# Three-layer compressed interaction network on one core: the field products in four strips of 32 rows instead of two halves of 64, two of them in banks of y

## The chip, the cores and the metric

The kernel runs on one core of a Trainium2 chip. The metric is the device time of one execution in microseconds; before the change its median over three runs is 1070.07 us (1069.95 to 1070.9). The core has five engines that run their own queues and wait for each other by semaphores: TensorE (matmuls, PE in the profile, its weight loads PEld), VectorE (DVE), ScalarE (ACT), GpSimd (POOL) and SyncE (SP, which issues most DMAs). Matmuls write to PSUM, which has eight banks of 512 f32 values a partition; VectorE and ScalarE read and write it.

## The reference

```python
# r_input: (512, 64, 16) = batch, fields, embedding; W0: (128, 64*64); W1, W2: (128, 128*64)
x_vec = input
outs = []
for W, b in [(W0, b0), (W1, b1), (W2, b2)]:
    z = einsum('bhd,bfd->bhfd', x_vec, input)      # every row of x_vec times every field
    z = z.reshape(B, h * f, d)
    x_vec = einsum('oc,bcd->bod', W, z) + b[None, :, None]
    outs.append(x_vec.sum(axis=2))                 # sum over the embedding
return concatenate(outs, axis=1)                   # (512, 384)
```

All values are float32.

## The kernel before

**Tiles.** A column is a pair of batch element and embedding place. A tile is 128 columns (TILE_B = 8 batch elements of 16 places), a group is four tiles, and there are 16 groups, so 64 tiles. `body` runs once for the first group, in a sequence for the 14 inner groups, and once for the last.

**Layer 0** (`layer0`) makes l0 = W0 z for a whole group in 17 steps t. z, the products of fields, is made by GpSimd (`product`) from copies that DMAs lay down shifted. Nine of the steps are "in parts" (PARTED): z is split in an upper part (ScalarE, `part_upper`) and a remainder (VectorE, `part_lower`), and three fast matmuls take the place of a two-pass one. The steps of group n+1 are done while group n is in layer 1: AHEAD_AT lists behind which of the group's 64 chunks each stands, PARTED_AT when ScalarE and VectorE split.

**Layer 1** is the bulk. For each tile TensorE makes 16 chunks (`chunk`): chunk c holds the products of the tile's columns with W1 for four fields (CF = 4), 512 values a partition, in three matmuls of 512 columns (`by_parts`). A chunk lands in one of five banks y[0..4], taken in turn: chunk c of a tile waits until chunk c - 5 has been taken out. Taking out means: multiply each field's 128 columns by the field's value of the column and add. There are three ways. A chunk in SUMMED is done by VectorE in four multiply-adds into acc (`add_fields`). A chunk in SCALED is multiplied in place by ScalarE (`scale`, four activations) and added by VectorE in one step. A chunk in HELPED is multiplied by ScalarE into prod (`multiply`) and added up by GpSimd in pacc (`add_products`). HELPED is (1, 4, 6, 8, 12), SCALED (3,), and (3, 9) in the last four tiles. After the tile GpSimd adds acc and pacc to x2 (`combine`), in the last tile VectorE does.

**Field products.** For layer 2 the kernel doesn't form z again. For each tile it makes gram, for every batch element the products of x2's rows with the fields, summed over the embedding. The columns of a batch element must not mix, so `own_rows` lays the fields in bd once per batch element of a half, zero where a column isn't its own: HALF_B = 4 copies of 64 columns by four activations, and 4 columns more for the plain sums. `layer2` is two f32 matmuls, rows 0 to 63 and rows 64 to 127 of the tile, each 260 columns wide, into the two banks l2p[0] and l2p[1]. It is done for tile - 1 behind chunk LAYER2_AT = 13 of a tile. ScalarE copies both banks out with one copy to gram and one to sums1 (`layer2_out`, behind chunk 14's place). Every 16 tiles `quarter` multiplies gram by W2 on TensorE; the last quarter comes at the end of the kernel.

**Order.** Nothing plans: every engine's order is the program's, by the index e = 16 j + c of a chunk in its group. ScalarE also copies W2 in 16 parts (`keep_w2`, at chunk indices 78, 89, ... 243 of the kernel). At the end TensorE keeps busy with 24 transposes, waits for x2 of tile 63, makes its field products and the last quarter.

Of the kernel before, what the change touches and what calls it, by code (L numbers as in the profile page):

```python
# [7 lines left out]
ALU = mybir.AluOpType  # L8
# [5 lines left out]
O = 128  # L14
# [5 lines left out]
HALF = P // 2  # L20
HALF_B = TILE_B // 2
# [44 lines left out]
OWN_AT = 11  # L66
GRAM = HALF_B * F

# [4 lines left out]
LOWER_AT = 3  # L73
# [15 lines left out]
LATER_AT = [3 + t * 11 // ZT for t in range(ZT)]  # L89
# [3 lines left out]
LATER_PRODUCTS = (6, (3, 0, 5, 3, 0))  # L93
AHEAD_AT = [8 + t * 46 // (ZT - 1) for t in range(ZT)]
# [22 lines left out]
def cin_kernel(nc, x, w0, b0, w1, b1, w2, b2, out):  # L117
    with ExitStack() as ctx:
        def sb(name, shape, dt=F32):
            return ctx.enter_context(nc.sbuf_tensor(name, shape, dt))  # L120
# [23 lines left out]
        bd = sb("bd", [P, 2, GRAM + HALF_B])  # L144
# [6 lines left out]
        own_half = sb("own_half", [P, HALF_B])  # L151
# [32 lines left out]
        beside = GRAM + HALF_B  # L184
# [331 lines left out]
        def _(act):  # L516
# [150 lines left out]
            def own_rows(tile, j):  # L667
# [17 lines left out]
            def multiply(tile, j, c):  # L685
# [36 lines left out]
            nc.scalar.copy(gram[:, :, QB - TILE_B:QB - HALF_B], l2p[:, 0, 0:GRAM].rearrange("p (b f) -> p f b", f=F))  # L722
            nc.scalar.copy(sums1[:, B - TILE_B:B - HALF_B], l2p[:, 0, GRAM:GRAM + HALF_B]).then_inc(l2p_used, 1)
# [5 lines left out]
        def _(dve):  # L729
# [37 lines left out]
            def add_fields(tile, j, c):  # L767
# [4 lines left out]
                if c in scaled_in(tile):  # L772
# [3 lines left out]
                    nc.vector.tensor_tensor(to, y[(CHUNKS * tile + c) % YB][:], to, ALU.add).then_inc(acc_step, 1)  # L776
# [141 lines left out]
            for k in range(W1_AHEAD):  # L918
# [14 lines left out]
            nc.vector.tensor_copy(gram[:, :, QB - HALF_B:QB],  # L933
                                  l2p[:, 1, 0:GRAM].rearrange("p (b f) -> p f b", f=F)).then_inc(gram_half_made, 1)
# [251 lines left out]
```

## Time and profile before

| | us |
|---|---|
| median of three runs | 1070.07 |
| lowest, highest | 1069.95, 1070.9 |
| the profiled execution | 1069.11 |
| its span, first to last instruction | 1067.4 |
| TensorE busy | 1049.3 |
| VectorE busy | 916.8 |
| GpSimd busy | 874.4 |
| ScalarE busy | 672.8 |
| granted TensorE clock, mean | 1.000 |

Busy means that at least one instruction of the engine was on its way. The rows stand in a section of their own below. In a row of a timeline come the start in us from the span's start, the duration in us, the engine, the line, the operation, what it writes and reads, and how many records were merged; in brackets the idle time of the engine ahead of it and the engine and line that ended it. The lines that matter: L951 are the three matmuls of a chunk (and of a step in parts), L972 a whole step of layer 0, L1065 the field products, L1147 the transposes that keep TensorE busy, L1158 the last quarter, L1051 the other quarters, L791 VectorE's multiply-add, L776 its one-step sum of a scaled chunk, L814 a bias step on sums0, L693 ScalarE's multiply into prod, L682 its scale in place, L672 the rows of `own_rows`, L581 and L722 its copies to gram, L615 the copy of W2.

### The profile page before, as it was taken

Reading aid. Unit: us, or ns where it says so; the run is one execution under the profiler, and the core shown is the slowest. Engines: PE = TensorE matmul, PEld = TensorE weight load, DVE = VectorE, ACT = ScalarE, POOL = GpSimd, SP = SyncE. Lnnn points to the kernel's source line nnn. Section 1 sums busy time; section 2 is a strip of 40 time slices with the busy share of each in tenths; the row PEclk is TensorE's granted clock in tenths of the full one; section 3 lists DMA queues with packets and bytes.
Section 4 is the critical chain, followed back from the end, with each engine's and each line's share of the span. In section 5 each row is a group of like instructions: output and inputs, shape, how many; then the busy total and the mean of one; then the engine's idle time right before and its main releaser. Section 6 shows DMA issues by size and latency. Waiting matters only on the chain.

```text
span 1067.4 us, 18145 instructions
## 1 busy us (share of the span) xinstructions
PE 1049.3 (98%) x4764; PEld 803.3 (75%) x4764; DVE 916.8 (86%) x2874; ACT 672.8 (63%) x2253; POOL 874.4 (82%) x727
## 2 busy tenths in 40 slices
PE   6999999999999999999999999999999999999998
PEld 6866777777787777777778777777778877777777
DVE  5988989898966999989993898989997599998983
ACT  4756677786744756666563665767565475766771
POOL 2789998989886898989985899898988589898660
PEclk9999999999999999999999999999999999999999
DMA  7443435354321433223141241423332133331000
GB/s 280 102 120 86 112 84 130 87 119 107 80 61 48 85 84 77 80 59 98 50 105 43 40 112 53 97 80 70 100 77 60 47 70 92 75 79 41 1 24 8
DMA packets 124105, 85.96 MB, mean 81 GB/s; under 512 B 87585, under 2 KB 90625, under 8 KB 123873
## 3 DMA queue, kind: packets, MB, share of 16 engines
q1 hardware_dynamic: 105968, 74.04, 28.8%
q10 hardware_dynamic: 18032, 10.75, 3.3%
q8 instruction: 38, 0.62, 0.2%
q14 instruction: 67, 0.54, 0.2%
HBM read 14.81 MB, written 0.79 MB: 15 GB/s over the span
## 4 chain that ended last, share of the span: by engine, by line
PE 89%; DVE 4%; POOL 3%; issue 2%; DMA 1%; ACT 1%; ACTq 0%; DVEq 0%; POOLq 0%
PE y L951 60%; PE l L951 9%; PE l L972 9%; PE l2p L1051 4%; PE l2p L1065 3%; DVE acc L791 3%; PE l2p L1158 1%; DMA gram<-in_L_rec_W_dram 1%; POOL z L465 1%; POOL pacc L475 1%; PE l2p L1006 1%; POOL pacc L473 1%; PE l2p L1029 1%; POOL pacc L481 0%; ACT y L682 0%
## 5 line engine op out<-in xcount | busy, mean ns | idle before, releaser
L791 DVE SCALAR_TENSOR_TENSOR acc<-y,x0t,acc 128x128 f32<-128x128 f32 x2288 | 619.8, 339 | 90.2 <-PE y L951 86.6
L693 ACT ACTIVATE prod<-y,x0t 128x128 f32<-128x128 f32 x1280 | 368.0, 379 | 284.9 <-PE y L951 221.8
L951 PE MATMUL y<-w1h,x1h 128*128 128x512 f32 x1024 | 451.1, 440 | 2.9 <-issue 1.5
L951 PE MATMUL y<-w1h,x1l 128*128 128x512 f32 x1024 | 400.6, 391 | 0.0
L951 PE MATMUL y<-w1l,x1h 128*128 128x512 f32 x1024 | 399.9, 390 | 0.0
L465 POOL TENSOR_TENSOR z<-z,xg 128x512 f32<-128x512 f32 (+2 forms) x272 | 361.5, 1334 | 22.0 <-DMA z<-xg 22.0
L475 POOL TENSOR_TENSOR pacc<-pacc,prod 128x512 f32<-128x512 f32 x192 | 271.0, 1412 | 68.5 <-ACT prod L693 64.4
L951 PEld LDWEIGHTS y<-w1h,x1h 128*128 128x128 f32 x1024 | 192.9, 188 | 77.5 <-DVE acc L791 19.8
L951 PEld LDWEIGHTS y<-w1l,x1h 128*128 128x128 f32 x1024 | 192.6, 188 | 59.2 <-issue 25.2
L951 PEld LDWEIGHTS y<-w1h,x1l 128*128 128x128 f32 x1024 | 192.2, 188 | 42.0
L740 DVE TENSOR_TENSOR zl<-z,zh 128x512 fp32r<-128x512 f32 (+1 forms) x144 | 144.3, 1003 | 5.4 <-ACT zh L542 5.2
L473 POOL TENSOR_TENSOR pacc<-prod 128x512 f32<-128x512 f32 x64 | 85.5, 1336 | 37.8 <-ACT prod L693 37.3
L972 PE MATMUL l<-z,w0t 128*128 128x512 f32 (+1 forms) x224 | 114.4, 592 | 0.0
L481 POOL TENSOR_TENSOR pacc<-pacc,acc 128x512 f32<-128x512 f32 x63 | 86.8, 1378 | 31.1 <-DVE acc L791 30.8
L542 ACT CAST zh<-z 128x512 fp32r<-128x512 f32 (+1 forms) x144 | 90.7, 630 | 13.3 <-POOL z L465 12.7
L682 ACT ACTIVATE y<-y,x0t 128x128 f32<-128x128 f32 x272 | 76.4, 351 | 14.7 <-PE y L951 14.7
L672 ACT ACTIVATE bd<-x0t,own_half 128x64 f32<-128x64 f32 x256 | 69.7, 373 | 1.0 <-ACT w2t L615 1.0
L776 DVE TENSOR_TENSOR acc<-y,acc 128x512 f32<-128x512 f32 x68 | 46.8, 688 | 24.3 <-ACT y L682 23.4
L951 PE MATMUL l<-zh,w0h 128*128 128x512 f32 (+1 forms) x144 | 58.8, 408 | 1.3 <-DVE zl L740 1.3
L483 POOL TENSOR_TENSOR pacc<-pacc 128x256 f32<-128x256 f32 x63 | 55.4, 880 | 4.9
L951 PE MATMUL l<-zl,w0h 128*128 128x512 f32 (+1 forms) x144 | 55.8, 388 | 0.0
L951 PE MATMUL l<-zh,w0l 128*128 128x512 f32 (+1 forms) x144 | 55.8, 387 | 0.0
(102 smaller groups left out, 698.5 us busy)
## 6 DMA issues: line engine op xcount, KB each, us to landing
z<-xg SPq DMA_DIRECT2D x480, 128.0 KB, 2.4
w2t<-in_L_rec_W_dram ACTq DMA_DIRECT2D x8, 512.0 KB, 10.3
sums<-in_L_rec_W_dram ACTq DMA_DIRECT2D x16, 256.0 KB, 4.0
xg<-in_r_input_dram SPq DMA_DIRECT2D x30, 128.0 KB, 3.9
z<-xg SPq DMA_DIRECT2D x32, 96.0 KB, 2.2
z<-xg SPq DMA_DIRECT2D x15, 192.0 KB
gram<-in_L_rec_W_dram ACTq DMA_DIRECT2D x1, 2048.0 KB, 10.4
out_dram<-z SPq DMA_DIRECT2D x3, 192.0 KB, 1.9
```

The costliest lines, as they stand in the source:

```text
L465: nc.gpsimd.tensor_tensor(to[0:rows, :], to[0:rows, :], xg[0:rows, cols], ALU.mult).then_inc(z_made, 1)
L473: nc.gpsimd.tensor_tensor(pacc[:], prod[:, 0], prod[:, 1], ALU.add).then_inc(pool_step, 1)
L475: nc.gpsimd.tensor_tensor(pacc[:], pacc[:], prod[:, h % HSLOTS], ALU.add).then_inc(pool_step, 1)
L481: nc.gpsimd.tensor_tensor(pacc[:], pacc[:], acc[:, slot], ALU.add).then_inc(pool_step, 1)
L542: nc.scalar.copy(zh[:, slot, cols], zin(n, t)).then_inc(zh_made, 1)
L672: last = nc.scalar.activation(bd[:, j % 2, b * F:(b + 1) * F], x0t[:, j, :], ACT.Copy, scale=own_half[:, b:b + 1])
L682: last = nc.scalar.activation(of, of, ACT.Copy, scale=x0t[:, j, f:f + 1])
L693: last = nc.scalar.activation(prod[:, h % HSLOTS, k, :], y[(CHUNKS * tile + c) % YB][:, k * O:(k + 1) * O], ACT.Copy, scale=x0t[:, j, f:f ...
L740: nc.vector.tensor_tensor(zl[:, i % ZLSLOTS, cols], zin(n, t), zh[:, zhslot(n, t), cols].bitcast(F32), ALU.subtract).then_inc(zl_made, 1)
L791: ins = nc.vector.scalar_tensor_tensor(out=to, in0=of, scalar=x0t[:, j, f:f + 1], in1=b1r[:] if m == 0 else to, op0=ALU.mult, op1=ALU.add)
L951: ins = nc.tensor.matmul(to, stationary, moving, start=(first and k == 0), stop=(last and k == 2))
L972: nc.tensor.matmul(l0[:, cols], w0t[:, WHOLE.index(t), :], zin(n, t), start=(t == 0), stop=False).then_inc(z_used, 1)
```

## The change

The tile is cut in four strips of 32 rows (STRIPS, STRIP, STRIP_B = 2) where it was cut in two halves. bd is 2 x 64 + 2 = 130 columns wide and `own_rows` makes two copies in place of four, now at chunk 4 (OWN_AT) in place of 11. `layer2` issues four matmuls of 32 rows and 130 columns: the first two into l2p[0] and l2p[1], the others into two banks of y. These two count as turns in y's rotation, so a tile has 18 turns: 14 chunks, two strips, two chunks. `ybank`, `turn_of`, `strip_turns` and `user_ahead` work out whose turn a bank had before, and `turn_free` is the wait for it. `layer2_out` copies the strips out in three pairs of copies in place of one. In the last tile ScalarE copies two strips and VectorE two.

The rest is a new deal: HELPED becomes (0, 4, 6, 9, 12), SCALED (3, 11) and (3,) in the last group. Lists of places follow (AHEAD_AT, AHEAD_FIRST_AT, LATER_AT, PARTED_FIRST_AT, PRODUCTS_AT, LOWER_AT), with nine steps in parts as before. AHEAD_AT was 8, 10, 13, 16, 19, 22, 25, 28, 31, 33, 36, 39, 42, 45, 48, 51, 54 and becomes 10, 12, 15, 18, 21, 24, 26, 29, 32, 35, 38, 40, 43, 46, 49, 52, 55; the last of LATER_AT goes from 13 to 14.

```diff
-HALF = P // 2
-HALF_B = TILE_B // 2
+STRIPS = 4
+STRIP = P // STRIPS
+STRIP_B = TILE_B // STRIPS
-HELPED = (1, 4, 6, 8, 12)
+HELPED = (0, 4, 6, 9, 12)
-SCALED = (3,)
-SCALED_LAST = (3, 9)
+SCALED = (3, 11)
+SCALED_LAST = (3,)
-OWN_AT = 11
-GRAM = HALF_B * F
+OWN_AT = 4
+GRAM = STRIP_B * F
-LOWER_AT = 3
+LOWER_AT = 2
-LATER_AT = [3 + t * 11 // ZT for t in range(ZT)]
+LATER_AT = [3 + t * 12 // ZT for t in range(ZT)]
-LATER_PRODUCTS = (6, (3, 0, 5, 3, 0))
-AHEAD_AT = [8 + t * 46 // (ZT - 1) for t in range(ZT)]
+LATER_PRODUCTS = (5, (3, 0, 5, 4, 0))
+AHEAD_AT = [10 + t * 45 // (ZT - 1) for t in range(ZT)]
-AHEAD_FIRST_AT = [26 + t * 29 // (ZT - 1) for t in range(ZT)]
+AHEAD_FIRST_AT = [27 + t * 28 // (ZT - 1) for t in range(ZT)]
-PARTED_FIRST_AT = [{AHEAD_FIRST_AT[t] - k: t for t in PARTED} for k in (5, 3)]
+PARTED_FIRST_AT = [{AHEAD_FIRST_AT[t] - k: t for t in PARTED} for k in (5, 4)]
-PRODUCTS_FIRST_AT = ((0, 0, 0, 0, 0), (0, 3, 1, 0, 1), (3, 3, 1, 1, 4), (0, 0, 0, 0, 0))
-PRODUCTS_AT = ((2, 1, 1, 1, 1), (1, 1, 1, 1, 1), (1, 1, 1, 1, 1), (1, 0, 0, 0, 0))
+PRODUCTS_FIRST_AT = ((0, 0, 0, 0, 0), (0, 4, 1, 1, 1), (3, 2, 1, 1, 3), (0, 0, 0, 0, 0))
+PRODUCTS_AT = ((2, 1, 1, 1, 1), (2, 1, 1, 1, 1), (1, 1, 1, 1, 1), (0, 0, 0, 0, 0))
...
+        Y_STRIPS = STRIPS - 2
+        TURNS = CHUNKS + Y_STRIPS
+        def turn_of(tile, c):
+            return TURNS * tile + c + (Y_STRIPS if c > LAYER2_AT else 0)
+        def ybank(tile, c):
+            return turn_of(tile, c) % YB
+        def strip_turns(tile):
+            first = TURNS * tile + (LAYER2_AT + 1 if tile < GROUPS * TILES else 0)
+            return range(first, first + Y_STRIPS)
+        def user_ahead(turn):
+            tile, at = divmod(turn - YB, TURNS)
+            if LAYER2_AT < at <= LAYER2_AT + Y_STRIPS:
+                return (tile, None) if tile > 0 else user_ahead(turn - YB)
+            return tile, at - (Y_STRIPS if at > LAYER2_AT else 0)
...
             def layer2_out(tile, to):
-                nc.scalar.copy(gram[:, :, bass.ds(to, TILE_B)].rearrange("p f (k b) -> p f k b", k=2),
-                               l2p[:, :, 0:GRAM].rearrange("p k (b f) -> p f k b", f=F))
-                nc.scalar.copy(sums1[:, bass.ds(tile * TILE_B, TILE_B)].rearrange("p (k b) -> p k b", k=2),
-                               l2p[:, :, GRAM:GRAM + HALF_B]).then_inc(l2p_used, 1)
+                parts = [(0, l2p[:], 2)]
+                parts += [(2 + i, y[turn % YB][:].unsqueeze(1), 1) for i, turn in enumerate(strip_turns(tile + 1))]
+                for at, of, k in parts:
+                    b = at * STRIP_B
+                    nc.scalar.copy(gram[:, :, bass.ds(to + b, k * STRIP_B)].rearrange("p f (k b) -> p f k b", k=k),
+                                   of[:, :, 0:GRAM].rearrange("p k (b f) -> p f k b", f=F))
+                    last = nc.scalar.copy(
+                        sums1[:, bass.ds(tile * TILE_B + b, k * STRIP_B)].rearrange("p (k b) -> p k b", k=k),
+                        of[:, :, GRAM:GRAM + STRIP_B])
+                last.then_inc(l2p_used, 1)
...
             def own_rows(tile, j):
-                for b in range(HALF_B):
+                for b in range(STRIP_B):
...
+            def turn_free(turn):
+                user, c = user_ahead(turn)
+                if c is None:
+                    pe.wait_ge(l2p_used, user + 1)
+                elif user < 0:
+                    return
+                elif c in HELPED:
+                    pe.wait_ge(prod_made, HN * user + HN + HELPED.index(c) + 1)
+                else:
+                    pe.wait_ge(acc_step, added(user, c))
...
             def layer2(tile, slot, fields_kept, quarters_out):
-                for k in range(2):
-                    half = slice(k * HALF, (k + 1) * HALF)
-                    last = nc.tensor.matmul(l2p[:, k, 0:GRAM + HALF_B], x2[half, slot], bd[half, slot, :],
+                turns = strip_turns(tile + 1)
+                for turn in turns:
+                    turn_free(turn)
+                for k, to in enumerate([l2p[:, 0], l2p[:, 1]] + [y[turn % YB][:] for turn in turns]):
+                    rows = slice(k * STRIP, (k + 1) * STRIP)
+                    last = nc.tensor.matmul(to[:, 0:GRAM + STRIP_B], x2[rows, slot], bd[rows, slot, :],
                                             start=True, stop=True)
                 last.then_inc(l2p_made, 1)
             def chunk(tile, j, c):
-                before, late = (c - YB) % CHUNKS, c < YB
-                if before in HELPED:
-                    value = HN * tile + (HN + HELPED.index(before) + 1) - (HN if late else 0)
-                    pe.wait_ge(prod_made, value)
-                else:
-                    pe.wait_ge(acc_step, added(tile - 1 if late else tile, before))
+                turn_free(turn_of(tile, c))
```

## Rows read from the trace of the kernel before

**Rows 1.** The page, busy time, share of the span and instructions of each engine

```profile
PE 1049.3 (98%) x4764; PEld 803.3 (75%) x4764; DVE 916.8 (86%) x2874; ACT 672.8 (63%) x2253; POOL 874.4 (82%) x727
```

**Rows 2.** The page, the chain that ended last, by engine and by line

```profile
PE 89%; DVE 4%; POOL 3%; issue 2%; DMA 1%; ACT 1%; ACTq 0%; DVEq 0%; POOLq 0%
PE y L951 60%; PE l L951 9%; PE l L972 9%; PE l2p L1051 4%; PE l2p L1065 3%; DVE acc L791 3%; PE l2p L1158 1%; DMA gram<-in_L_rec_W_dram 1%; POOL z L465 1%; POOL pacc L475 1%; PE l2p L1006 1%; POOL pacc L473 1%; PE l2p L1029 1%; POOL pacc L481 0%; ACT y L682 0%
```

**Rows 3.** Groups by line and form: busy us, mean ns, then idle before

```profile
L791 DVE SCALAR_TENSOR_TENSOR acc<-y,x0t,acc 128x128 f32<-128x128 f32 x2288 | 619.8, 339 | 90.2 <-PE y L951 86.6
L951 PE MATMUL y<-w1h,x1h 128*128 128x512 f32 x1024 | 451.1, 440 | 2.9 <-issue 1.5 <-DVE acc L791 0.9 <-ACT prod L693 0.3
...
L672 ACT ACTIVATE bd<-x0t,own_half 128x64 f32<-128x64 f32 x256 | 69.7, 373 | 1.0 <-ACT w2t L615 1.0
...
L1051 PE MATMUL l2p<-gram,w2t 128*128 128x128 f32 x384 | 46.7, 275 | 0.0
...
L581 ACT COPY gram<-l2p 128x512 f32<-128x512 f32 x63 | 37.4, 594 | 12.1 <-PE l2p L1065 11.5 <-ACT w2t L615 0.4
...
L615 ACT COPY w2t<-sums 128x512 f32<-128x512 f32 x16 | 18.6, 1164 | 0.0
```

**Rows 4.** Timeline, TensorE and ScalarE around one tile's field products, in narrow windows

```profile
511.09 0.39 PE L951 MATMUL y<-w1h,x1l 128*128 128x512 f32 x1
511.40 0.49 PE L1065 MATMUL l2p<-bd,x 64*128 64x260 f32 x2
511.73 0.39 PE L1065 MATMUL l2p<-bd,x 64*128 64x260 f32 x2
...
512.16 0.59 ACT L581 COPY gram<-l2p 128x512 f32<-128x512 f32 x1 [0.35 <-PE l2p L1065]
512.38 0.39 PE L951 MATMUL y<-w1l,x1h 128*128 128x512 f32 x1
```

**Rows 5.** Timeline, last thirds of two chunks and the multiply one releases

```profile
540.82 0.39 PE L951 MATMUL y<-w1h,x1l 128*128 128x512 f32 x1
...
541.25 1.15 ACT L693 ACTIVATE prod<-y,x0t 128x128 f32<-128x128 f32 x4 [0.40 <-PE y L951]
...
541.50 0.39 PE L951 MATMUL y<-w1h,x1l 128*128 128x512 f32 x1
```

**Rows 6.** Timeline, a scaled chunk of the last tile, all three engines

```profile
1039.85 0.39 PE L951 MATMUL y<-w1h,x1l 128*128 128x512 f32 x1
...
1040.09 1.14 ACT L682 ACTIVATE y<-y,x0t 128x128 f32<-128x128 f32 x4
...
1041.25 0.69 DVE L776 TENSOR_TENSOR acc<-y,acc 128x512 f32<-128x512 f32 x1 [1.35 <-ACT y L682]
```

**Rows 7.** Timeline, TensorE waiting for a bank early in the last group

```profile
999.75 1.14 DVE L814 TENSOR_SCALAR sums<-sums,b0d 128x512 f32<-128x512 f32 x1
1000.81 1.11 DVE L791 SCALAR_TENSOR_TENSOR acc<-y,x0t,acc 128x128 f32<-128x128 f32 x4
...
1001.98 0.50 PE L951 MATMUL y<-w1h,x1h 128*128 128x512 f32 x1 [0.88 <-DVE acc L791]
...
1002.31 0.39 PE L951 MATMUL y<-w1l,x1h 128*128 128x512 f32 x1
```

**Rows 8.** Busy time of each engine (records) in group 14 and last group

```profile
933.90:994.10 60.20, 60.20 (x255) 45.09 (x254) 55.93 (x179) 39.62 (x136) 54.79 (x45) 1.00 0.20 54
994.10:1044.30 50.20, 49.17 (x218) 37.26 (x217) 44.37 (x153) 38.38 (x141) 30.33 (x28) 1.00 0.04 13
```

**Rows 9.** Timeline, the end of the last tile

```profile
1042.05 5.26 DVE L791 SCALAR_TENSOR_TENSOR acc<-y,x0t,acc 128x128 f32<-128x128 f32 x20
...
1044.10 0.40 PE L951 MATMUL y<-w1h,x1l 128*128 128x512 f32 x1
...
1048.94 0.71 PE L1065 MATMUL l2p<-bd,x 64*128 64x260 f32 x4 [1.83 <-DVE x L929]
1049.70 0.37 ACT L722 COPY gram<-l2p 128x256 f32<-128x256 f32 x1 [5.93 <-PE l2p L1065]
```

More of the change, by code:

```diff
@@ L183, in cin_kernel @@
         l2p = ps("l2p", [P, 2, CHUNK])
-        beside = GRAM + HALF_B
+        beside = GRAM + STRIP_B
         l2 = l2p[:, 0, beside:beside + QB]
@@ L680, in scale @@
                     f = CF * c + k
-                    of = y[(CHUNKS * tile + c) % YB][:, k * O:(k + 1) * O]
+                    of = y[ybank(tile, c)][:, k * O:(k + 1) * O]
                     last = nc.scalar.activation(of, of, ACT.Copy, scale=x0t[:, j, f:f + 1])
@@ L692, in multiply @@
                     f = CF * c + k
-                    last = nc.scalar.activation(prod[:, h % HSLOTS, k, :], y[(CHUNKS * tile + c) % YB][:, k * O:(k + 1) * O],
+                    last = nc.scalar.activation(prod[:, h % HSLOTS, k, :], y[ybank(tile, c)][:, k * O:(k + 1) * O],
                                                 ACT.Copy, scale=x0t[:, j, f:f + 1])
@@ L721, in _ @@
             act.wait_ge(l2p_made, layer2_ready(GROUPS * TILES - 1))
-            nc.scalar.copy(gram[:, :, QB - TILE_B:QB - HALF_B], l2p[:, 0, 0:GRAM].rearrange("p (b f) -> p f b", f=F))
-            nc.scalar.copy(sums1[:, B - TILE_B:B - HALF_B], l2p[:, 0, GRAM:GRAM + HALF_B]).then_inc(l2p_used, 1)
+            nc.scalar.copy(gram[:, :, QB - TILE_B:QB - 2 * STRIP_B].rearrange("p f (k b) -> p f k b", k=2),
+                           l2p[:, :, 0:GRAM].rearrange("p k (b f) -> p f k b", f=F))
+            nc.scalar.copy(sums1[:, B - TILE_B:B - 2 * STRIP_B].rearrange("p (k b) -> p k b", k=2),
+                           l2p[:, :, GRAM:GRAM + STRIP_B]).then_inc(l2p_used, 1)
             act.wait_ge(turned, B // P)
@@ L775, in add_fields @@
                     to = acc[:, j % 2].rearrange("p k o -> p (k o)")
-                    nc.vector.tensor_tensor(to, y[(CHUNKS * tile + c) % YB][:], to, ALU.add).then_inc(acc_step, 1)
+                    nc.vector.tensor_tensor(to, y[ybank(tile, c)][:], to, ALU.add).then_inc(acc_step, 1)
                     return
@@ L781, in add_fields @@
                     f = CF * c + k
-                    to, of = acc[:, j % 2, k, :], y[(CHUNKS * tile + c) % YB][:, k * O:(k + 1) * O]
+                    to, of = acc[:, j % 2, k, :], y[ybank(tile, c)][:, k * O:(k + 1) * O]
                     if after_scaled and k == 0:
@@ L837, in _ @@
             dve.wait_ge(consts_made, 1)
+            by_strip = own[:].rearrange("p (k b) -> p b k", b=STRIP_B)
             for slot in range(2):
-                nc.vector.tensor_tensor(bd[:, slot, GRAM:GRAM + HALF_B], own[:, 0:HALF_B], own[:, HALF_B:TILE_B], ALU.add)
-            nc.vector.tensor_tensor(own_half[:], own[:, 0:HALF_B], own[:, HALF_B:TILE_B], ALU.add).then_inc(own_made, 1)
+                nc.vector.tensor_reduce(bd[:, slot, GRAM:GRAM + STRIP_B], by_strip, AX.X, ALU.add)
+            nc.vector.tensor_reduce(own_strip[:], by_strip, AX.X, ALU.add).then_inc(own_made, 1)
             dve.wait_ge(x_turned, 1)
@@ L932, in _ @@
             dve.wait_ge(l2p_made, layer2_ready(tile))
-            nc.vector.tensor_copy(gram[:, :, QB - HALF_B:QB],
-                                  l2p[:, 1, 0:GRAM].rearrange("p (b f) -> p f b", f=F)).then_inc(gram_half_made, 1)
-            nc.vector.tensor_copy(sums1[:, B - HALF_B:B], l2p[:, 1, GRAM:GRAM + HALF_B]).then_inc(gram_half_made, 1)
+            strip_banks = [y[turn % YB] for turn in strip_turns(tile + 1)]
+            for i, of in enumerate(strip_banks):
+                at = QB - (Y_STRIPS - i) * STRIP_B
+                last = nc.vector.tensor_copy(gram[:, :, at:at + STRIP_B],
+                                             of[:, 0:GRAM].rearrange("p (b f) -> p f b", f=F))
+            last.then_inc(gram_half_made, 1)
+            for i, of in enumerate(strip_banks):
+                at = B - (Y_STRIPS - i) * STRIP_B
+                last = nc.vector.tensor_copy(sums1[:, at:at + STRIP_B], of[:, GRAM:GRAM + STRIP_B])
+            last.then_inc(gram_half_made, 1)
             dve.wait_ge(b2r_made, 1)
```

8 lines of the change are left out of this document (4 added, 4 removed).

## The prediction

> **What bounds the kernel now.** I read the page's busy shares, then the chain of waits, then the groups by line, then timelines of single tiles. TensorE is busy 98% of the span at a granted clock of 1.00 and carries 89% of the chain; VectorE is at 86% [rows 1, 2]. Busy time alone isn't proof, so look at the idle column: before the 1024 first matmuls of the chunks TensorE idled 2.9 us in all, and the clean groups of sixteen chunks are 60.2 us of 60.2 busy [rows 3, 8]. From tile 4 on, the time is the sum of what TensorE streams. A third of a chunk takes 0.227 us (541.50 less 540.82, over three) [rows 5], a chunk 0.68 us. VectorE fills 55.9 of 60.2 us of such a group and ScalarE 39.6 [rows 8]: neither ends last, but VectorE has only 4.3/4 = 1.1 us of slack a tile. So the change can gain only by shortening the TensorE stream, and it loses wherever TensorE comes to wait.
>
> **Field products (`layer2`), 64 times.** Before, they are two matmuls of 64 rows and 260 columns, four records each time (two passes a matmul). What they cost is read from the starts: the last third of the chunk before starts at 511.09 and would end at 511.32; the second third of the next chunk starts at 512.38 where 511.55 would be its undisturbed start: 0.83 us [rows 4]. Its parts: 0.08 us until the first weights load (511.32 to 511.40), about 0.10 us of load that nothing covers (the first pair reads 0.49 us, the second 0.39) [rows 4], then two pairs of passes, then the same two gaps on the way back. The two halves run side by side: two records start within one printed hundredth at 511.40, two at 511.73 [rows 4], and ScalarE's copy starts at 512.16, 0.43 us behind the second pair's start. From an ordinary third, 540.82, to the multiply that it releases, 541.25, it is 0.43 as well [rows 4, 5], so the second pair streams no longer than an ordinary third and nothing is queued behind it. Two pairs take 0.83 - 4 x 0.10 = 0.43 us, 0.217 each for 260 columns.
>
> After, four matmuls of 32 rows and 130 columns. If all four strips run side by side, there are again two waves, of 130 columns: 0.108 each, 0.22 together; the load for the second wave (0.10) just fits under the first. The gain is 0.21 us a time. Bounds: nothing at all, if only two strips run at once (four waves of 0.108); a loss of 0.50 if the eight passes ran singly, at 46.7/384 = 0.12 us for a pass of 128 columns [rows 3], which the pairs of [rows 4] speak against. Issue isn't the limit as far as a row shows it: the records of a pair start together [rows 4]. I take 0.21, the row nearest in kind: 64 x 0.21 = **-13.4 us**. The Trainium skill (TensorE: Matmul & The Clock Gate, "Measured speedup vs the span model") gives four row strips 3.07 times the speed of one after another, not 4; by that the waves would be 8 x 0.108/3.07 = 0.28 us, an estimate, and the sum 4 us less of a gain. No row here shows four strips, and the sum leaves it out.
>
> **Banks of y.** This is the price. The last two strips take two turns of the five banks between chunks 13 and 14. Chunk 14 then needs chunk 11 out of its bank (before: 9), chunk 15 needs 12, the next tile's chunk 0 needs 13, and the products need 9 and 10. Queued behind such a wait is all of TensorE. From the end of chunk 11's stream to chunk 14's lie two chunks and the products: 0.68 + 0.68 + 0.62 = 1.98 us. Chunk 11 is now scaled in ScalarE and added in one VectorE step. Its consumption is priced from such a chunk of the last tile: third started 1039.85, stream end 1040.08, scale starts at 1040.09 when ScalarE was late, or 0.20 behind the stream's end when it is free (0.43 less 0.23) [rows 5, 6]; from scale start to the end of the sum 1041.94 - 1040.09 = 1.85. So 0.20 + 1.85 = 2.05. The release itself, read at the one stall of the last group: VectorE ends at 1001.92, the next third starts at 1001.98 and its second at 1002.31, so it really streamed from 1002.08: 0.16 [rows 7]. Chunk 14 can stream at 2.21 behind chunk 11 where it could at 1.98: a stall of 0.2 us, unless a step of the first layer lies between. The new list AHEAD_AT puts one behind chunks 12 (tile 0 of a group), 13 (tile 1) and 11 (tile 2), each 0.68 us or more, and none behind chunk 7 of tile 3. So 15 tiles pay: 15 x 0.2 = **+3 us**. The other new limits hold by my working of tile 3: chunk 9 (1.35 behind its end by rows of 1.15 us a multiply plus 0.20), 10 (1.6 behind, by laying VectorE's steps in program order from chunk 13 of tile 2 on; limit 2.0), 13 (limit 1.98 + 0.2) and the strips themselves: ScalarE's six copies, 1.1 us by an estimate from 0.59 for 512 columns and 0.37 for 256 [rows 3, 9], end 2.2 us behind chunk 13's end, against 2.8 for chunk 1 of the next tile.
>
> **ScalarE.** It adds a scaled chunk (1.14 us) [rows 6], saves two of the four rows of `own_rows` (69.7/256 = 0.27 each) and gets 0.35 us more of copies: +0.95 us in a tile of 15, on an engine at 66% [rows 3, 8]: hidden. Not hidden are the sixteen 1.16 us copies of W2 (L615) [rows 3] where one meets a tight chunk without a step behind it. They fall at indices 78, 89, ... 243: index 122 is chunk 10 of a tile 3, ahead of the scaled chunk 11 (1.1 us late), and 188 is chunk 12 of a tile 3 (0.8 us); the other fourteen meet a step of layer 0 or a wait of full depth. **+1.9 us**; 0 to 6 as bounds.
>
> **VectorE and GpSimd.** VectorE saves four steps of 619.8/2288 = 0.27 and adds one of 0.69: -0.4 us a tile [rows 3, 6]. No time by itself; it is why chunk 10 is soon free. GpSimd does the same 17 products and five sums a tile; the sum of the first two still waits for chunk 4, while its slot is now wanted at chunk 9 instead of 8, so that wait shrinks. The extra waits in TensorE's queue (two) are hidden: its sequencer passes them ahead of the stream.
>
> **First and last group.** In tile 0 the last step of layer 0 moves from behind chunk 13 to behind chunk 14, and with it the values that tile 1 starts on; against it, VectorE has 0.4 us less a tile there. I take +0.5, bounds -1.5 and +2.5. The last group has no steps of layer 0: 64 chunks and four products stream 46 us, and VectorE needs 4 x (10 x 1.07 + 0.65) + 2 = 47.4 us. Before, the 50.2 us of [rows 8] less 43.5 and 3.3 left 3.4 us for row turns and stalls, 1.1 of it at chunk 10 of its first tile, behind the bias step of 1.14 us [rows 7]. With a tighter rotation I put 0.5 on top. But VectorE then ends nearer behind the last chunk: chunk 11 can be 1.8 us behind at most (1.98 less the release), and by 1.07 a chunk 15 is then some 1.9 behind. Before, VectorE ended at 1047.31, 3.0 us behind the last chunk's stream (1044.33), and TensorE waited 1.83 us for x2 [rows 9]: -1.1. The second copies of the last two strips cost under 0.1.
>
> **Sum.** -13.4 + 3.0 + 1.9 + 0.5 + 0.5 - 1.1 = -8.6 us. The profiled execution took 1069.11 us (span 1067.4), 0.96 under the median of the runs; from it the sum gives 1060.5, and put on the median 1070.07 - 8.6 = **1061.5 us**.
>
> **Rivals.** (a) Two strips at a time. Two records start at once in this trace, never three [rows 4]. Then the products cost 0.83 as before, the 13.4 is gone and the +4.8 of the rest stays: 1074.9 us, slower. It decides as soon as fewer than some 0.08 us a tile are gained. The Trainium skill (TensorEngine Tiling (Array Packing), "Tiling Modes") lists four tiles of 32 rows by 128 columns as working independently; by that rule this rival falls, and nothing in this trace can show it. (b) Full concurrency, but the short rotation stalls every tile, not the last of each group alone, because VectorE (93% of a group) comes late to chunks 10 and 13 when its steps for layer 0 lie there: 49 more tiles x 0.19 = 9.3, 1070.8 us, no change. For it speaks that VectorE was 3.0 us behind the last chunk [rows 9]; against it that it has 0.4 us less to do and a step of layer 0 stands in each of these places. (c) No stall at all: chunk 11's sum keeps up, 1061.5 - 4.9 - 0.5 = 1056 us.
>
> **Chances.** Forecast 0.56 (1059 to 1066), (c) 0.12, (b) 0.17, (a) 0.15. The likeliest one's time is the prediction. The range reaches from just under (c), 1055.5, to just under (a), 1074.0; it leaves out most of (a), some 0.13, and some 0.04 below. A measurement of this kernel tells 0.2% (2.1 us) from no change. Faster than 1067.9: the forecast, (c) and 0.02 of (b), 0.70. Within: 0.12 of (b). Slower: (a) and 0.03 of (b), 0.18.
>
> **What would show it.** In the changed trace the eight records of a tile's products start in two bunches of four about 0.11 us apart, and next chunk's second third is back 0.21 us sooner, with 0.62 us for the whole. Four bunches of two mean rival (a). Idle time before the first third of chunk 14, in tile 3 of a group alone, of 0.2 us and released by VectorE's one-step sum, shows the bank price; in all tiles, rival (b). A clean group should last 60.2 - 0.84 + 0.2 = 59.6 us. The last products' wait for x2 should fall from 1.8 to about 0.7 us. The prediction is wrong if the strips don't overlap, if strips' copies hold chunk 1, or if the retimed first group loses more than 2.5 us.

## The result and the profile after

The changed kernel takes 1080.42 us (median of four runs, 1079.6 to 1080.92) against 1070.01 us of the kernel before (median of four runs). The ratio is 1.0099, 95% interval 1.0087 to 1.0112: about 1% slower, and outside the range that was given (1055.5 to 1074.0 us). The profiled execution took 1079.6 us.

| | before | after |
|---|---|---|
| span, us | 1067.4 | 1077.8 |
| TensorE busy | 1049.3 | 1042.3 |
| VectorE busy | 916.8 | 923.4 |
| ScalarE busy | 672.8 | 708.2 |
| GpSimd busy | 874.4 | 867.2 |

The page first: busy times and the chain by engine, which answer to [rows 1, 2]. (The shares of the chain add up to 78% here, so they are a rough guide.)

```profile
PE 1042.3 (97%) x5020; PEld 803.1 (75%) x5020; DVE 923.4 (86%) x2708; ACT 708.2 (66%) x2601; POOL 867.2 (80%) x727
...
PE 61%; DVE 13%; issue 4%; ACT 0%; POOL 0%; DVEq 0%; ACTq 0%
```

TensorE has 7 us less to do and carries 61% of the chain where it carried 89%; VectorE went from 4% to 13%. VectorE issues 166 instructions fewer and is busy 7 us longer. The groups by line and form say where (busy us, mean ns):

```profile
L772 DVE TENSOR_TENSOR zl<-z,zh 128x512 fp32r<-128x512 f32 x135 | 157.5, 1167 | 1.7 <-ACT zh L566 1.7
...
L780 DVE TENSOR_TENSOR zh<-z,zh 32x512 fp32r<-32x512 f32 x15 | 20.0, 1334 | 0.5
```

These are `part_lower` and `left_lower`, the same instructions as before, where they took 1012 and 1002 ns:

```profile
L740 DVE TENSOR_TENSOR zl<-z,zh 128x512 fp32r<-128x512 f32 x135 | 136.6, 1012 | 3.8 <-ACT zh L542 3.7
...
L748 DVE TENSOR_TENSOR zh<-z,zh 32x512 fp32r<-32x512 f32 x15 | 15.0, 1002 | 0.5
```

Who held TensorE up (waited for: us in total, times, longest; counted from the modelled end of the matmul before, so a little less than by the starts used below):

```profile
PE l L1000 <- DVE zh L780: 13.3, 10, 1.4
PE y L991 <- DVE acc L808: 4.8, 11, 1.4
```

L1000 is layer 0's last step, L808 VectorE's one-step sum of a scaled chunk. A clean group and the last one, as in [rows 8]:

```profile
946.00:1007.50 61.50, 59.90 (x271) 45.04 (x270) 56.21 (x166) 42.26 (x160) 54.69 (x45) 1.00 0.18 48
1007.50:1056.20 48.70, 47.86 (x235) 37.68 (x235) 46.53 (x168) 33.82 (x133) 30.82 (x29) 1.00 0.04 13
```

The group lasts 61.5 us, TensorE has 59.9 us of work in it. The last group is 1.5 us shorter than before.

**What went as forecast.** The field products, which answer to [rows 4], with the thirds of chunks around them:

```profile
500.77 0.39 PE L991 MATMUL y<-w1h,x1l 128*128 128x512 f32 x1
501.09 0.38 PE L1120 MATMUL l2p<-bd,x 32*128 32x130 f32 x2
501.11 0.38 PE L1120 MATMUL y<-bd,x 32*128 32x130 f32 x2
501.31 0.28 PE L1120 MATMUL l2p<-bd,x 32*128 32x130 f32 x2
501.32 0.28 PE L1120 MATMUL y<-bd,x 32*128 32x130 f32 x2
501.53 0.50 PE L991 MATMUL y<-w1h,x1h 128*128 128x512 f32 x1
501.86 0.39 PE L991 MATMUL y<-w1l,x1h 128*128 128x512 f32 x1
```

The eight records come in two bunches of four, all four strips at once. The bunches start 0.22 us apart and not 0.11 as the prediction's sign had it: that figure left out the 0.10 us of weight load that its own sum counts. The next chunk's second third starts at 501.86 where 501.23 would be undisturbed (500.77 plus two thirds of 0.227): 0.63 us, 0.20 less than 0.83. (In the clean groups the products cost 0.84 us before and 0.63 to 0.65 us now, in whichever tile they stand.)

**What did not.** In tile 3 of a group TensorE stands still for 1.56 us: a third starts at 419.71 and is streamed by 419.94, and the step behind it starts at 421.50. VectorE, GpSimd and TensorE in one stretch, in the order of engines:

```profile
411.85 2.44 DVE L772 TENSOR_TENSOR zl<-z,zh 128x512 fp32r<-128x512 f32 x1
...
419.85 1.59 DVE L780 TENSOR_TENSOR zh<-z,zh 32x512 fp32r<-32x512 f32 x1
...
411.20 1.29 POOL L489 TENSOR_TENSOR z<-z,xg 96x512 f32<-96x512 f32 x1
412.46 1.28 POOL L499 TENSOR_TENSOR pacc<-pacc,prod 128x512 f32<-128x512 f32 x1
...
419.63 1.26 POOL L497 TENSOR_TENSOR pacc<-prod 128x512 f32<-128x512 f32 x1 [0.17 <-POOL x L510]
...
419.71 0.40 PE L991 MATMUL y<-w1h,x1l 128*128 128x512 f32 x1
421.50 0.51 PE L1000 MATMUL l<-zh,w0left 96*128 96x512 f32 x1 [1.39 <-DVE zh L780]
```

Read it from the end. TensorE's step starts at 421.50, 0.06 us behind the end of VectorE's left part (421.44). The left part took 1.59 us; GpSimd's sum, which was running when it started, ended at 420.89, 0.55 us before it. Eight us earlier, the eighth `part_lower` of the group (t = 14) took 2.44 us. It started while GpSimd's last product ran, that one ended at 412.49, and the part-lower did not get on then: GpSimd's next sum went first and ended at 413.74, 0.55 us before the part-lower's end at 414.29. Everything that VectorE does behind it is later by what it lost.

**The account.** From the starts of all chunks in both traces: the first chunk starts 0.7 us sooner, the first 15 groups take 14.1 us more, the last 1.6 less, the end behind the last third 1.4 less: +10.4 us of span. In the 15 groups the wait at layer 0's last step comes to 16.0 us (1.5 to 1.7 us in ten groups, none in five, among them the three inner ones in which a quarter gives VectorE time), the wait at chunk 14 of tile 3 to 6.4 us. The shorter products give back 60 x 0.20 = 12.0 us of that. The 3.7 us left over are smaller waits, those at W2's copies among them, and some 0.15 us a group that TensorE's stream got longer with the new lists.

### The profile page after: what moved, and what is told of

Same layout as the page of the kernel before. It is cut to its first block, busy times and chain, and to the rows that moved or that the text cites. A ratio compares the mean times of both kernels' runs of the same rounds, so it can differ in the third digit from the quotient of the medians.

```text
span 1077.8 us, 18897 instructions
## 1 busy us (share of the span) xinstructions
PE 1042.3 (97%) x5020; PEld 803.1 (75%) x5020; DVE 923.4 (86%) x2708; ACT 708.2 (66%) x2601; POOL 867.2 (80%) x727
## 4 chain that ended last, share of the span: by engine, by line
PE 61%; DVE 13%; issue 4%; ACT 0%; POOL 0%; DVEq 0%; ACTq 0%
PE y L991 42%; DVE acc L823 9%; PE l L1012 6%; PE l L991 6%; PE l2p L1091 4%; DVE acc L808 2%; DVE zl L772 2%; PE l2p L1208 1%; PE l2p L1120 1%; DVE acc L821 1%; PE l2p L1069 0%; ACT y L712 0%; POOL pacc L505 0%; DVE x1l L789 0%; PE l L1079 0%
## 5 line engine op out<-in xcount | busy, mean ns | idle before, releaser
L823 DVE SCALAR_TENSOR_TENSOR acc<-y,x0t,acc 128x128 f32<-128x128 f32 x2064 | 561.4, 340 | 72.3 <-PE y L991 64.7
L723 ACT ACTIVATE prod<-y,x0t 128x128 f32<-128x128 f32 x1280 | 363.3, 382 | 207.8 <-PE y L991 150.3
L712 ACT ACTIVATE y<-y,x0t 128x128 f32<-128x128 f32 x496 | 138.4, 345 | 96.3 <-PE y L991 95.5
L772 DVE TENSOR_TENSOR zl<-z,zh 128x512 fp32r<-128x512 f32 (+1 forms) x144 | 166.6, 1157 | 1.7 <-ACT zh L566 1.7
L808 DVE TENSOR_TENSOR acc<-y,acc 128x512 f32<-128x512 f32 x124 | 85.4, 689 | 45.8 <-ACT y L712 40.0
L497 POOL TENSOR_TENSOR pacc<-prod 128x512 f32<-128x512 f32 x64 | 82.9, 1295 | 19.6 <-ACT prod L723 18.6
L566 ACT CAST zh<-z 128x512 fp32r<-128x512 f32 (+1 forms) x144 | 95.1, 661 | 2.7 <-POOL z L489 2.6
L821 DVE TENSOR_SCALAR acc<-y,x0t 128x128 f32<-128x128 f32 x192 | 54.7, 337 | 0.0
L507 POOL TENSOR_TENSOR pacc<-pacc 128x256 f32<-128x256 f32 x63 | 50.4, 800 | 4.9
```

The source lines that it names most:

```text
L497: nc.gpsimd.tensor_tensor(pacc[:], prod[:, 0], prod[:, 1], ALU.add).then_inc(pool_step, 1)
L566: nc.scalar.copy(zh[:, slot, cols], zin(n, t)).then_inc(zh_made, 1)
L712: last = nc.scalar.activation(of, of, ACT.Copy, scale=x0t[:, j, f:f + 1])
L723: last = nc.scalar.activation(prod[:, h % HSLOTS, k, :], y[ybank(tile, c)][:, k * O:(k + 1) * O], ACT.Copy, scale=x0t[:, j, f:f + 1])
L772: nc.vector.tensor_tensor(zl[:, i % ZLSLOTS, cols], zin(n, t), zh[:, zhslot(n, t), cols].bitcast(F32), ALU.subtract).then_inc(zl_made, 1)
L808: nc.vector.tensor_tensor(to, y[ybank(tile, c)][:], to, ALU.add).then_inc(acc_step, 1)
```

## The experiments

The first theory, P: what is lost comes from VectorE's steps for layer 0 meeting GpSimd's operations, at the places that the new lists give them. Its rivals: R, the two banks fewer are the loss by themselves; V, VectorE simply has too much to do there.

**The strips alone.**

```diff
-HELPED = (0, 4, 6, 9, 12)
-SCALED = (3, 11)
-SCALED_LAST = (3,)
+HELPED = (1, 4, 6, 8, 12)
+SCALED = (3,)
+SCALED_LAST = (3, 9)
...
-AHEAD_AT = [10 + t * 45 // (ZT - 1) for t in range(ZT)]
+AHEAD_AT = [8 + t * 46 // (ZT - 1) for t in range(ZT)]
```

(and every other list as before, on the changed kernel)

> Four strips and their two turns in y's banks, with the deal of chunks and all lists of before. Theory P (the loss of the change comes from the new places: VectorE's eighth part-lower of a group and its left part meet GpSimd's sums back to back, take 2.44 and 1.59 us in place of 0.95 each, and layer 0's last step waits 1.67 us for them, twelve groups long; the strips themselves gain 0.21 us a tile): the wait at the last step of layer 0 isn't there, the gain of 13 us is, and chunks 10 and 11, both VectorE's here, cost about 0.9 us in the last tile of a group: some 1070 us. Rival R (two banks fewer are the loss, whatever the deal): with chunks 9, 10 and 11 all VectorE's the rotation is at its worst, every tile stalls by 0.3 us or more, over 1080 us.

Measured: 1078.59 us, ratio 1.0079 (1.0064 to 1.0094). Neither theory's number. The wait at layer 0's last step isn't there, but a clean group is 60.6 us: the rotation costs it some 1.1 us, 0.7 at chunk 14 and 0.3 at chunk 0 of its last tile. Most of all it costs in the last group, 54.3 us where it was 50.2:

```profile
939.60:1000.20 60.60, 59.93 (x271) 45.00 (x270) 56.88 (x178) 38.96 (x144) 54.47 (x45) 1.00 0.20 54
1000.20:1054.50 54.30, 48.12 (x234) 37.82 (x233) 45.97 (x156) 37.62 (x149) 30.57 (x28) 1.00 0.04 12
```

With chunks 9, 10 and 11 all for VectorE to take out, TensorE waits for it; the waits of this kernel name the multiply-adds:

```profile
PE y L991 <- DVE acc L823: 9.7, 22, 0.9
PE l2p L1120 <- DVE acc L823: 5.6, 14, 1.1
```

So the strips need the new deal. R's mechanism is real with the old deal, but not in every tile as R had it: in a clean group it shows around the last tile alone.

**The deal alone.** The kernel before with all the lists of the change, two halves and five banks.

```diff
-HELPED = (1, 4, 6, 8, 12)
-SCALED = (3,)
-SCALED_LAST = (3, 9)
+HELPED = (0, 4, 6, 9, 12)
+SCALED = (3, 11)
+SCALED_LAST = (3,)
...
-AHEAD_AT = [8 + t * 46 // (ZT - 1) for t in range(ZT)]
+AHEAD_AT = [10 + t * 45 // (ZT - 1) for t in range(ZT)]
```

> Two halves as before, full rotation of five banks, with the new deal of chunks and all new lists. Theory P: the eighth part-lower is late here too, the wait of about 1.6 us at the last step of layer 0 stands in twelve groups or so, and no 13 us are gained: 1085 to 1092 us. Rival R: with the five banks back there is no loss, 1070 us or less.

Measured: 1074.62 us, ratio 1.0045 (1.0028 to 1.0062), ten less than P said and over R's 1070. The eighth part-lower is late here too, 2.24 us at the median of nine clean groups, but the left part takes 0.68 us, and the last step waits 0.18 us and not 1.56. The same places don't bring the whole loss: with other lengths on TensorE, the late part-lower still meets two operations, but the left part meets other work.

**GpSimd's sums cut short**, in the changed kernel and in the one before. Three of the four sums into pacc of a tile add a quarter of their columns and leave out the rest.

```diff
-nc.gpsimd.tensor_tensor(pacc[:], pacc[:], prod[:, h % HSLOTS], ALU.add)
+nc.gpsimd.tensor_tensor(pacc[:, 0:1], pacc[:, 0:1], prod[:, h % HSLOTS, 0:1], ALU.add)
```

> The changed kernel with GpSimd's three later sums of a tile (L499) cut from 512 columns to 128; the rest of these sums is left out, so the result lacks three parts of it. Everything else is as in the change. Theory P: VectorE no longer waits for GpSimd's sums, its eighth part-lower takes under 1.4 us, the wait at the last step of layer 0 falls from 1.67 us to under 0.3, a clean group lasts some 59.8 us and not 61.5: 1060 to 1065 us. Rival R, and rival V (VectorE has simply too much to do in tiles 2 and 3, or waits for ScalarE): 1078 to 1081 us as the change.

> The kernel before with GpSimd's three later sums of a tile cut to 128 columns (three parts of these sums are left out). It is the control for the run that cut them in the change. Theory P: there TensorE waits for nothing that VectorE was held up in, so it gains under 2 us: 1068 to 1070 us. If short sums speed up any kernel of this form by themselves, 1055 us or less.

Measured: the changed kernel falls to 1063.68 us (0.994, 0.9926 to 0.9955), with the eighth part-lower and the left part at 0.68 us each and no wait at the last step. That looked like proof. The control spoils it: the kernel before with the same cut goes up to 1081.85 us (1.0107, 1.0092 to 1.0122), where I had expected no change. A clean group there is 61.25 us, with waits of 0.58 and 0.30 us at layer 0's last two steps, behind chunks 3 and 6 of tile 3. VectorE comes late to them: its seventh part-lower takes 1.72 us (0.77 in the full kernel), and the eighth 1.63 (0.95 in the full kernel), because it meets a product as that begins:

```profile
410.14 1.63 DVE L740 TENSOR_TENSOR zl<-z,zh 128x512 fp32r<-128x512 f32 x1
...
409.93 1.29 POOL L465 TENSOR_TENSOR z<-z,xg 96x512 f32<-96x512 f32 x1
```

(409.93 + 1.29 = 411.22, and 411.77 is again 0.55 us later.) Less work on GpSimd doesn't take the meetings away, it shifts them. The pair shows that the phase between the two engines is worth 10 us and more in either direction; it doesn't show that taking GpSimd's time away helps, nor by itself which meeting the change loses its time to.

**Layer 0's steps spread wider**, so that the last is at chunk 57 and not 55.

```diff
-AHEAD_AT = [10 + t * 45 // (ZT - 1) for t in range(ZT)]
+AHEAD_AT = [10 + t * 47 // (ZT - 1) for t in range(ZT)]
```

> The changed kernel with the steps of layer 0 spread wider (AHEAD_AT ends at 57, not 55; all that hangs on it moves too). Theory P: the last step no longer waits, or under 0.5 us; what stays is 0.2 to 0.4 us at chunk 14 of the last tile of a group: 60.1 us a group, 1062 to 1068 us. Rival R: the wait moves to the banks, 1076 us or more. Rival V: half of the wait stays, some 1072 us.

Measured: 1072.40 us, ratio 1.0019 (1.0009 to 1.0028). That is V's number, but not its mechanism: no half of the wait stays. The wait at the last step is gone in clean groups and the eighth part-lower takes 0.68 us; a clean group is 60.4 us, where P had 60.1. What is left there is 0.24 us at a group's first chunk, and chunk 14, which has lost its step of layer 0 in tile 1, and waits 0.27 us in tile 1 and 0.44 in tile 3. Outside the clean groups the first group is 2.4 us longer than in the run below. The waits of the whole kernel for VectorE's one-step sums:

```profile
PE y L991 <- DVE acc L808: 9.1, 26, 1.0
```

**One VectorE instruction moved.** The clean test: the eighth part-lower stands one chunk later, nothing else is touched.

```diff
-PARTED_AT = [{AHEAD_AT[t] - k: t for t in PARTED} for k in (5, 4)]
+PARTED_AT = [{AHEAD_AT[t] - k + (1 if t == 14 and k == 4 else 0): t for t in PARTED} for k in (5, 4)]
```

> The changed kernel with one VectorE instruction a group moved by one chunk: the eighth part-lower (t = 14) stands behind chunk 14 of tile 2 and not behind chunk 13, in the fourteen inner groups. Theory P (it meets GpSimd's back-to-back work there and is held for it): its duration falls from 2.45 us to 1.2 or less, the wait at the last step of layer 0 from 1.6 us to at most 0.2, a clean group from 61.5 us to some 60.0, and the time to 1060 to 1066 us. Rival V (VectorE has too much to do ahead of the last step, wherever its steps stand): 1077 us or more.

Measured: 1062.36 us, ratio 0.9937 (0.9922 to 0.9952): 18 us less than the change, and faster than before. The time is P's, though the part-lower fell to 1.38 us and not to 1.2. VectorE's steps there (the 0.68 at 412.32 is the moved one's successor, t = 15, the 0.68 at 415.90 the left part) and GpSimd's:

```profile
409.99 1.38 DVE L772 TENSOR_TENSOR zl<-z,zh 128x512 fp32r<-128x512 f32 x1
411.29 1.12 DVE L823 SCALAR_TENSOR_TENSOR acc<-y,x0t,acc 128x128 f32<-128x128 f32 x4
412.32 0.68 DVE L772 TENSOR_TENSOR zl<-z,zh 128x512 fp32r<-128x512 f32 x1
...
415.90 0.68 DVE L780 TENSOR_TENSOR zh<-z,zh 32x512 fp32r<-32x512 f32 x1
...
408.28 1.29 POOL L489 TENSOR_TENSOR z<-z,xg 96x512 f32<-96x512 f32 x1
409.54 1.28 POOL L499 TENSOR_TENSOR pacc<-pacc,prod 128x512 f32<-128x512 f32 x1
```

The moved instruction now meets the fourth sum (ends 410.82) and nothing behind it: 1.38 us where it took 2.44. The left part starts in a gap of GpSimd's, 415.51 to 416.52, and no wait is left at layer 0's last step. V is out: VectorE has the same work. A clean group lasts 59.8 us:

```profile
930.70:990.50 59.80, 59.66 (x272) 44.98 (x271) 55.26 (x166) 42.28 (x160) 54.47 (x46) 1.00 0.19 51
```

**One GpSimd instruction moved.** The run before changed the order of VectorE's steps as well, so this one leaves VectorE alone.

```diff
-PRODUCTS_AT = ((2, 1, 1, 1, 1), (2, 1, 1, 1, 1), (1, 1, 1, 1, 1), (0, 0, 0, 0, 0))
+PRODUCTS_AT = ((2, 1, 1, 1, 1), (2, 1, 1, 1, 1), (1, 1, 1, 1, 0), (1, 0, 0, 0, 0))
```

> The changed kernel with VectorE's order untouched; GpSimd's last product of a group (t = 16) stands at the start of tile 3, behind its fourth sum, and not between its third and fourth sum of tile 2. Theory P (VectorE's eighth part-lower is held until GpSimd has no operation in a row behind the one it met): the part-lower meets one operation at most and takes 1.0 to 1.4 us in place of 2.45, the wait at layer 0's last step falls from 1.6 us to 0.5 or less, a clean group from 61.5 us to 60.5 or less, and the time to 1062 to 1070 us. Rival O (what helped in the run that moved one was VectorE's order, chunk 14's sum ahead of the part-lower, and not what GpSimd did): the wait stays at 1.2 us or more, 1076 us or more.

Measured: 1062.55 us, ratio 0.9927 (0.9911 to 0.9944). VectorE's order is that of the change, and the loss is gone:

```profile
409.45 1.39 DVE L772 TENSOR_TENSOR zl<-z,zh 128x512 fp32r<-128x512 f32 x1
...
416.40 0.68 DVE L780 TENSOR_TENSOR zh<-z,zh 32x512 fp32r<-32x512 f32 x1
...
407.12 3.17 POOL L499 TENSOR_TENSOR pacc<-pacc,prod 128x512 f32<-128x512 f32 x2
410.25 1.74 POOL L489 TENSOR_TENSOR z<-z,xg 96x512 f32<-96x512 f32 x1
```

The part-lower starts 45.1 us into its group (45.0 in the change), meets the second sum of the row above it, which ends at 410.29, and ends 0.55 us behind it. This time GpSimd's next operation is the one held: the product takes 1.74 us in place of 1.29. Rival O is out. A clean group is as long as in the run before:

```profile
931.00:990.80 59.80, 59.66 (x272) 45.13 (x271) 55.30 (x166) 42.29 (x160) 55.01 (x46) 1.00 0.22 59
```

**The left part one chunk earlier**, the late part-lower left in place.

```diff
-LEFT_LOWER_AT = AHEAD_AT[-1] - 4
+LEFT_LOWER_AT = AHEAD_AT[-1] - 5
```

> The changed kernel with VectorE's left part moved one chunk earlier (behind chunk 2 and not 3 of tile 3), the eighth part-lower left where the change has it. Theory P: the part-lower stays at 2.4 us, but the left part misses GpSimd's first sum of the tile, takes 0.7 us and not 1.59 and is done about 1.4 us sooner; the wait at the last step falls from 1.6 to some 0.3 us, a clean group to 60.2 us, the time to 1063 to 1067 us. Rival V (VectorE has simply too much to do there): the order of two of its steps changes nothing at the end of both, the wait falls by under 0.5 us, 1075 us or more.

Measured: 1073.34 us, ratio 1.0027 (1.0018 to 1.0037), between the two theories' numbers; but V allowed the wait to fall by under 0.5 us, and it fell by 1.1. The part-lower still takes 2.35 us, the left part 0.95 in place of 1.59, and the wait at the last step falls from 1.56 to 0.48 us; but chunk 14 of tile 3 waits 0.70 us where it waited 0.40. What VectorE has lost turns up at the next tight place unless there is time to make it up.

**Two halves, with the part-lower moved.**

```diff
-PARTED_AT = [{AHEAD_AT[t] - k: t for t in PARTED} for k in (5, 4)]
+PARTED_AT = [{AHEAD_AT[t] - k + (1 if t == 14 and k == 4 else 0): t for t in PARTED} for k in (5, 4)]
```

(on the kernel of the deal alone)

> Two halves and five banks, with the new deal and lists, and the eighth part-lower moved as in the run that moved one. What the strips are worth alone then stands between the two runs: 0.21 us a tile less 0.2 us in every last tile, some 10 us. Theory P: 1070 to 1074 us here. If the strips' gain is smaller than read from the starts, under 1067 us.

Measured: 1072.18 us, ratio 1.0022 (1.0012 to 1.0031). Against 0.9937 of the run that moved one with four strips: the strips are worth 0.85%, 9.1 us net, 10 expected. This kernel with two halves is itself 0.22% slower than the kernel before: the new deal and lists cost some 2 us of their own, even with no late part-lower.

**Chunk 11 without the scale, and other places for layer 0's steps.** All three start from the wider spread.

```diff
-SCALED = (3, 11)
+SCALED = (3,)
```

> The kernel with the wider spread of layer 0's steps, and chunk 11 no longer scaled by ScalarE but summed by VectorE in four steps (SCALED is (3,)). Theory B (what is left of the loss there, some 0.8 us a group, is chunk 14 waiting for a scaled chunk 11 that is 2.05 us late at best, where 1.8 would do): the waits at chunk 14 of tiles 1, 2 and 3 (0.27, 0.19 and 0.45 us) fall under 0.1 each, a clean group goes from 60.4 to 59.7 us, and the time to 1060 to 1066 us. Rival D (VectorE's 0.4 us more a tile come out as waits instead): 1071 us or more.

Measured: 1073.12 us, ratio 1.0036 (1.0022 to 1.0050): the rival's number. Chunk 14's waits did fall, to nothing in tile 1 and 0.13 us in tile 3 (the 0.19 us that I had put on tile 2 was the length of the step there and no wait). But the first part-lower (t = 1) now takes 1.70 us where it took 0.75, TensorE waits 0.68 us for it in tile 0, and the group grows to 60.6 us. Whether VectorE's extra work does that, as the rival has it, or only a new meeting with GpSimd, this run doesn't separate. The waits for part-lowers:

```profile
PE l L991 <- DVE zl L772: 6.0, 13, 0.9
```

```diff
-AHEAD_AT = [10 + t * 47 // (ZT - 1) for t in range(ZT)]
+AHEAD_AT = [11 + t * 48 // (ZT - 1) for t in range(ZT)]
```

> As the one before, with layer 0's steps behind every third chunk from 11 to 59, so that tiles 0, 1 and 2 have one behind chunk 11, 13 and 12. Theory B: as the one before, 59.6 us a group, 1060 to 1065 us. If the steps come too late for the next group's first chunk, 0.5 to 1 us at each group's start: 1068 to 1075 us.

> Steps of layer 0 behind every third chunk from 11 to 59, with chunk 11 scaled as in the change. Theory B: the waits at chunk 14 are gone in tiles 0, 1 and 2, where a step stands between, and stay in tile 3 (0.2 to 0.4 us): a clean group 59.9 us, 1063 to 1067 us. Rival D: no difference to the run with the wider spread, 1072 us.

Measured: 1128.72 and 1128.36 us (1.0562 and 1.0555): both forecasts far off. The waits lie around the group's end, 1.4 us or so at each of the products in tiles 3 and 0 and at the group's first chunk. Ending at chunk 59, layer 0 probably leaves too little time for VectorE's lower part of the next x1; that is not shown, nor why it costs 4 us a group and not one.

**W2's copies two chunks later**, on top of the moved part-lower.

```diff
-W2_LOAD_AT = [CHUNKS * TILES + 4 + 11 * k for k in range(W2_PARTS)]
+W2_LOAD_AT = [CHUNKS * TILES + 6 + 11 * k for k in range(W2_PARTS)]
```

> The run that moved one part-lower, and W2's sixteen copies on ScalarE two chunks later each, so that none stands ahead of chunk 9, 10 or 11 of a last tile. Theory K (a W2 copy ahead of a tight chunk costs TensorE 0.3 to 1.3 us; 3.5 us in all in tiles 4 to 15): 1.5 to 3 us less than that run, 1059 to 1061 us. If the waits only move to other tiles: 1062 us as there.

Measured: 1060.56 us, ratio 0.9912 (0.9897 to 0.9927), the fastest of all. That is 1.8 us under the run without it; their intervals overlap. The trace shows why it isn't more: the waits in tiles 7, 8, 11 and 12 shrink, but a copy now stands ahead of chunk 10 of tile 14, and chunk 14 of that tile, which waited for nothing, waits 1.1 us.

## Why the prediction was wrong

By its own steps:

- **Products, -13.4 us.** Right. All four strips run at once. With three thirds around them they took 1.52 us before and take 1.32 now, 64 x 0.20 = 12.8 us; rival (a) is out.
- **Banks, +3 us.** Right in mechanism, place and size once the collisions are gone: with one instruction moved, chunk 14 waits 0.21 us in tile 3 of each clean group and nowhere else. In the change it waits 0.41, because VectorE comes to chunk 11 late. Rival (b), a wait in every tile, is out.
- **W2, +1.9 us.** Too small. In tiles 4 to 15 the run that moved one lost 3.5 us to these copies: 1.3 in tile 7 and 0.6 in tile 11 as forecast (1.1 and 0.8), and 1.1 and 0.3 in tiles 8 and 12, which I had put down as covered. In tile 8 it is again a meeting: ScalarE's upper part comes 1.2 us late behind the copy, VectorE's part-lower starts late and takes 1.78 us, and TensorE waits for it.
- **First group +0.5, last group -0.6.** Too careful. The first took 0.9 us less than before, the last with its end 3.0 less, of which the shorter products, counted above, are about 0.6 and 1.0. The wait for x2 in the last tile fell from 1.83 to 0.52 us; 0.7 was forecast.
- **"The other new limits hold by my working of tile 3."** This is the step that failed. I laid VectorE's steps in a row, each at one duration, and found chunk 10 out 1.6 us behind its end. And I asked only what chunks and strips wait for, not layer 0's last step, which waits for VectorE's left part. The mean of a part-lower before, 1.01 us, is a mean over meetings: by its place in the group it is 0.68 to 1.44 us there (medians of nine clean groups). Moving nine of them by one or two chunks against GpSimd draws these durations anew. In the change one drew 2.44 and the left part 1.59, which made 16.0 us of waits at the last step and 1.8 more at chunk 14: the whole distance to the 1062.4 us of the run without them.
- **"VectorE saves 0.4 us a tile. No time by itself."** The saving was eaten up. VectorE's busy time rose by 7 us, 22 of it in part-lowers (144.3 us before, 166.6 after).

In favour of the sum: without the collisions, the same kernel with one instruction elsewhere takes 1062.36 us where 1061.5 stood. By the ratio it gains 6.7 us where 8.6 were forecast, and part of that agreement is luck: the W2 term was 1.6 us too small and the new lists' own 2 us were not in the sum, while the first and last group gave back more than forecast. That doesn't make the forecast right. The change as it was made has the collisions, and I gave no chance to a loss from how VectorE and GpSimd meet, though [rows 8] show GpSimd busy 91% of a group.

## What to carry to other kernels

When steps are moved on an engine that shares a resource with another nearly full one, look at the spread of the step's durations by place, not at its mean: a spread of a factor of two says that the duration belongs to the meeting, and will be drawn anew by any move. After such a move look for the instruction that grew, and try it and its partner one place to either side before judging the idea; here that was worth 18 us, twice the idea itself. And a control on the kernel before belongs to each ablation: cutting GpSimd's sums "proved" the cause until the kernel before got slower by it.

## What the runs showed of the hardware

**VectorE's two-operand subtractions and GpSimd.** I took every record of `part_lower` outside the first group, 135 in each kernel. Those in which no GpSimd operation ends take 0.67 to 0.70 us. Those in which one does end 0.54 to 0.69 us behind its end, at a median of 0.55, in each of the fifteen traces of this case. In the change eleven were passed over once more and took up to 2.46 us; before and with one VectorE instruction moved there were none of these. VectorE's multiply-adds, which read one operand in PSUM, keep to 0.33 to 0.36 us in every trace. It works the other way too: GpSimd's operations of 1.29 us read 1.74 us when such a subtraction got in first. The Trainium skill (SBUF — State Buffer, "SBUF: two separate sides") says that VectorE, with two inputs in SBUF, and GpSimd, where it reads SBUF, share a port pair as an exclusive lock, held for a whole instruction by whoever starts first. These durations agree. It says nothing on who goes next when both wait: at 412.49 in the change GpSimd's next sum went ahead of a subtraction that had waited for 0.64 us, at 410.29 in the run that moved a product the subtraction went first. Over all fifteen traces a subtraction was passed over 47 times: 44 times it had met a product, three times the last small step of `combine`. It was never passed over behind one of the sums into pacc, though it met one with an operation right behind it 473 times. To meet a product isn't enough either: with a sum right behind, 41 of 529 such meetings were lost. Moving the one GpSimd product put a sum ahead of it where the product had stood ahead of the sum. Why the two differ stays open.

**Four strips.** Four f32 matmuls of 32 rows and 130 columns ran as two waves of four passes, 0.63 us with both changes of form; less the four gaps of 0.10 us that the prediction read, 0.23 us are left for the two waves, an estimate. The Trainium skill's measured factor of 3.07 for four row strips (TensorE: Matmul & The Clock Gate, "Measured speedup vs the span model"), measured there with 512 columns, would have given 0.68 us, an estimate (0.28 and the same gaps), and a full factor of four 0.62; the trace lies close to the latter. The Trainium skill (TensorEngine Tiling (Array Packing), "Key Properties") lets different tiles load and multiply in parallel, and the bunches of four agree.
